# Selective scan on Trainium2: GpSimd's share of the products of B and du taken from transfers that spread du over the partitions, 5 of 16 in place of 1 of 3

## The reference, cut to what matters

```python
deltaA = exp(delta[..., None] * A)            # per direction, channel, state
deltaBx = (delta * u)[..., None] * B          # du times B
h = deltaA * h_before + deltaBx               # recurrence along L, 16 states
y = sum over states of h * C
```

## Time and profile before

| | us |
|---|---|
| median of 3 runs | 28245.57 (28242.69 to 28276.12) |
| the profiled execution, its own time | 28245.18 |
| its span, first to last instruction | 28243.4 |
| VectorE busy | 25430.9 (90%) |
| PE matmuls busy | 23025.3 (82%) |
| GpSimd busy | 22840.0 (81%) |
| ScalarE busy | 14594.0 (52%) |
| mean granted TensorE clock | 0.841 |

### The profile page before, as it was taken

How to read it: one execution, slowest core, us unless ns; L and a number is a source line. 1 busy time by engine, 2 the same in 40 slices (tenths; PEclk the granted TensorE clock), 3 DMA queues, 4 the chain that set the end, 5 groups by cost and what they waited for, 6 DMA issues and landing times. The chain is left out here.

```text
span 28243.4 us, 328050 instructions
## 1 busy us (share of the span) xinstructions
PE 23025.3 (82%) x97488; PEld 6748.7 (24%) x97488; DVE 25430.9 (90%) x16259; ACT 14594.0 (52%) x20088; POOL 22840.0 (81%) x10240
## 2 busy tenths in 40 slices
PE   8878888888766888888887888888885788888886
PEld 3322222222232222222233222222222322222222
DVE  2489999999779999999986999999997799999998
ACT  1265555555366555555514655555552655555553
POOL 0169999999147999999971799999990499999993
PEclk9978888888777888888868888888887788888888
DMA  2242221221454222222266422122216622222224
GB/s 87 93 140 49 49 49 40 49 49 42 161 201 155 46 43 49 49 46 43 49 226 220 124 49 49 40 49 49 49 44 223 212 49 49 45 44 49 49 45 150
DMA packets 1123929, 2332.74 MB, mean 83 GB/s; under 512 B 98486, under 2 KB 609426, under 8 KB 1113868
## 3 DMA queue, kind: packets, MB, share of 16 engines
q1 hardware_dynamic: 1120340, 2308.66, 30.0%
q10 hardware_dynamic: 1728, 1.70, 0.0%
HBM read 1329.40 MB, written 980.58 MB: 82 GB/s over the span
## 5 line engine op out<-in xcount | busy, mean ns | idle before, releaser
L1589 POOL TENSOR_TENSOR scan_hc<-scan_bc,scan_h 128x1024 f32<-128x1024 f32 x6912 | 16069.3, 2356 | 123.7 <-DVE scan_h L1766 122.5
L1766 DVE TENSOR_TENSOR_SCAN scan_h<-scan_da,scan_state,scan_dbu 128x1024 f32<-128x1024 f32 x6912 | 15981.4, 2336 | 155.5 <-ACT scan_da L1643 147.3
L1680 PE MATMUL scan_da<-scan_dd,scan_ssel 32*128 32x512 f32 x27648 | 9125.4, 746 | 2994.8 <-DVE scan_h L1766 2760.6
L1643 ACT ACTIVATE scan_da<-scan_da,scan_a_cur 128x1024 f32<-128x1024 f32 x6912 | 7516.3, 1087 | 7752.1 <-PE scan_da L1680 7747.5
L1680 PE MATMUL scan_p_du<-scan_dd,scan_ssel 32*128 32x512 f32 x27648 | 9216.0, 746 | 451.7 <-DVE scan_dbu L1753 168.3
L1753 DVE TENSOR_TENSOR scan_dbu<-scan_p_du,scan_bc 128x1024 f32<-128x1024 f32 x4608 | 5553.8, 1205 | 370.2 <-PE scan_p_du L1680 336.1
L1575 POOL TENSOR_TENSOR scan_dbu<-scan_bc,scan_dus 128x1024 f32<-128x1024 f32 x2304 | 5431.4, 2357 | 58.7 <-ACT scan_dus L1617 56.5
L1680 PEld LDWEIGHTS scan_da<-scan_dd,scan_ssel 32*128 32x128 f32 x27648 | 2459.0, 217 | 10302.3 <-DVE scan_h L1766 8710.9
L1697 PE MATMUL scan_p_y<-scan_hc,scan_rsel 128*32 128x512 f32 x27648 | 4789.5, 774 | 18.4 <-POOL scan_hc L1589 17.8
L1680 PEld LDWEIGHTS scan_p_du<-scan_dd,scan_ssel 32*128 32x128 f32 x27648 | 2418.2, 212 | 3521.2 <-DVE scan_dbu L1753 2934.2
L1622 ACT ACTIVATE scan_state<-scan_h,scan_a_cur 128x1 f32<-128x1 f32 x6912 | 2023.4, 293 | 1571.6 <-DVE scan_h L1766 1462.0
(11 more groups left out here) (220 smaller groups left out, 13404.0 us busy)
## 6 DMA issues: line engine op xcount, KB each, us to landing
scan_bc<-bc_d SPq DMA_DIRECT2D x576, 512.0 KB, 12.0
du_d<-prep_useq SPq DMA_DIRECT2D x384, 576.0 KB, 3.7
delta_d<-prep_delta SPq DMA_DIRECT2D x384, 576.0 KB, 4.5
y_d<-scan_y SPq DMA_DIRECT2D x576, 384.0 KB, 5.2
scan_dd<-delta_d SPq DMA_DIRECT2D x1136, 192.0 KB, 4.8
scan_dd<-du_d SPq DMA_DIRECT2D x1136, 192.0 KB, 6.5
fin_y<-y_d SPq DMA_DIRECT2D x288, 576.0 KB, 5.2
xs_d<-proj_xs_o SPq DMA_DIRECT2D x96, 588.0 KB, 3.3
```

The lines of the kernel that those rows point to most:

```text
L1589: nc.gpsimd.tensor_tensor(hc[:, u % HC_SLOTS, :], c, h[:, u % H_SLOTS, :], ALU.mult).then_inc(hc_ready, 1)
L1643: nc.scalar.activation(da[u % DELTA_BANKS][:], da[u % DELTA_BANKS][:], ACT.Exp, scale=a_cur[:, slot(u)[0], u % UNITS:u % UNITS + 1]).then_ ...
L1680: return nc.tensor.matmul(dst[:, half * H:(half + 1) * H], ssel[rows, i, :], dd[rows, s, m, j, :], start=True, stop=True)
L1766: nc.vector.tensor_tensor_scan(h[:, v % H_SLOTS, :], da[v % DELTA_BANKS][:], dbu[:, v % DBU_SLOTS, :], state[:, v % UNITS:v % UNITS + 1], ...
```

## The change

GpSimd's share becomes 5 units of every 16 (u % 16 in 2, 5, 8, 11, 14), 15 to a chunk in place of 16. VectorE makes the other 11 of 16, 33 to a chunk in place of 32. For a shared unit TensorE spreads nothing and ScalarE copies nothing: SyncE issues one DMA (`load_share`) that reads the unit's 8 rows of du, 1024 positions each, 16 times over and writes all 128 partitions of one of 5 slots of `dus` (512 KB). It is issued when the product that held the slot is done, 5 shares ahead. SyncE's list for a chunk is now a sequence of 15 such steps, each with its wait for a product of GpSimd. The store of the chunk before, and the loads of the chunk after, stand behind the step k = STORE_AT = 6. ScalarE's `keep`, exponential and `evacuate`, with its wait above, are as they were. Before the first chunk, 5 share loads stand between `load_first` and the other loads (`load_rest`).

```diff
-TRIO = 3
+TURN = 16
+SHARED = (2, 5, 8, 11, 14)
+ROUND_SHARES = ROUND // TURN * len(SHARED)
+ROUND_OWN = ROUND - ROUND_SHARES
+SHARE_AHEAD = 4
 DELTA_BANKS = 2
 DBU_SLOTS = 6
-DUS_SLOTS = 2
+DUS_SLOTS = 5
+CHUNK_SHARES = UNITS // TURN * len(SHARED)
+STORE_AT = 6
 H_SLOTS = 4
 HC_SLOTS = 8
 PAIR = 2
...
-    return u % TRIO == 2
+    return u % TURN in SHARED
+
+
+def shares(u):
+
+    return len(SHARED) * (u // TURN) + sum(s < u % TURN for s in SHARED)
+
+
+def share_unit(k):
+
+    return k // len(SHARED) * TURN + SHARED[k % len(SHARED)]
...
-        share_spread = ph.sem("share_spread")
-        share_copied = ph.sem("share_copied")
+        dus_loaded = [ph.sem(f"dus_loaded{b}") for b in range(DUS_SLOTS)]
+        freed = ph.sem("freed")
...
+                def load_rest():
...
                     sp.wait_ge(y_ready, c * EIGHTS + EIGHTS + ONE)
+                    sp.sem_inc(freed, 1)
                     for half in range(2):
                         for b in range(2):
                             sp.dma_start(y_d[b * 64:(b + 1) * 64, :, bass.ds(at + half * H, H)],
                                          y[half * 64:(half + 1) * 64, b::2, :]).then_inc(y_stored, 16)
+                def load_share(at, k):
+                    m, j, i = unit(share_unit(k % CHUNK_SHARES))
+                    first = j * QUAD + i * CPU
+                    sp.dma_start(dus[:, k % DUS_SLOTS, :],
+                                 du_d[first:first + CPU, m, bass.ds(at, T)].unsqueeze(0).broadcast_to([STATES, CPU, T])).then_inc(dus_loaded[k % DUS_SLOTS], 16)
+
+                def chunk(c, at, s, first, last):
+
+
+                    for k in range(CHUNK_SHARES):
+                        ahead = k + DUS_SLOTS
+                        if ahead < CHUNK_SHARES or not last:
+
+                            sp.wait_ge(share_ready, c * CHUNK_SHARES + (k + 1) + ONE)
+                            sp.sem_inc(freed, 1)
+                            load_share(at + ahead // CHUNK_SHARES * T, ahead)
+                        if k == STORE_AT and not first:
+                            store(c - 1, at - T)
+                            if not last:
+                                load(at + T, 1 - s)
...
                 load_first()
-                for s in range(1, CHUNK_SLOTS):
-                    load(s * T, s)
-                with sp.Fori(0, (ALL_CHUNKS - CHUNK_SLOTS) // CHUNK_SLOTS) as i:
+                for k in range(DUS_SLOTS):
+                    load_share(0, k)
+                load_rest()
+                load(T, 1)
+                chunk(0, 0, 0, True, False)
+                with sp.Fori(0, (ALL_CHUNKS - 2) // CHUNK_SLOTS) as i:
                     for s in range(CHUNK_SLOTS):
-
-                        store(i * CHUNK_SLOTS + s, i * (CHUNK_SLOTS * T) + s * T)
-                        load(i * (CHUNK_SLOTS * T) + (s + CHUNK_SLOTS) * T, s)
-                for s in range(CHUNK_SLOTS):
-                    store(ALL_CHUNKS - CHUNK_SLOTS + s, (ALL_CHUNKS - CHUNK_SLOTS + s) * T)
+                        chunk(i * CHUNK_SLOTS + (s + 1), i * (CHUNK_SLOTS * T) + (s + 1) * T, 1 - s, False, False)
+                chunk(ALL_CHUNKS - 1, (ALL_CHUNKS - 1) * T, 1, False, True)
+                store(ALL_CHUNKS - 1, (ALL_CHUNKS - 1) * T)
...
-                def share(r, u):
-                    g.wait_ge(share_copied, r * (ROUND // TRIO) + (u // TRIO + 1) + ONE)
+                def share(r, u, first=False):
+                    if first and u == SHARED[0]:
+                        g.wait_ge(first_loaded, FIRST_LOADS + ONE)
+                    elif u % UNITS == SHARED[0] or first and FIRST_UNITS <= u < FIRST_UNITS + SHARE_AHEAD:
+
+                        t, n = slot(u)
+                        g.wait_ge(loaded[t], r * (TURNS * LOADS) + n * LOADS + ONE)
+                    k = shares(u)
+                    g.wait_ge(dus_loaded[k % DUS_SLOTS], r * (ROUND_SHARES // DUS_SLOTS * 16) + (k // DUS_SLOTS + 1) * 16 + ONE)
                     g.wait_ge(scanned, nth(r * ROUND, u - DBU_SLOTS + 1) + ONE)
                     g.sem_inc(passed, 1)
                     s, _ = slot(u % ROUND)
                     nc.gpsimd.tensor_tensor(dbu[:, u % DBU_SLOTS, :], bc[:, s, image(u % UNITS), :],
-                                            dus[:, u // TRIO % DUS_SLOTS, :], ALU.mult).then_inc(share_ready, 1)
...
-                        ahead = u + TRIO + 1
+                        ahead = u + SHARE_AHEAD
                         if shared(ahead) and not (last and ahead >= ROUND):
-                            share(r, ahead)
+                            share(r, ahead, first)
...
-                for u in range(TRIO):
-                    if shared(u):
-                        share(0, u)
-                rounds(0, False)
+                share(0, SHARED[0], True)
+                rounds(0, True, False)
...
-                def copy_share(r, u):
-                    a.wait_ge(share_spread, r * (ROUND // TRIO) + (u // TRIO + 1) + ONE)
-
-                    a.wait_ge(share_ready, nth(r * (ROUND // TRIO), u // TRIO - DUS_SLOTS + 1) + ONE)
-                    nc.scalar.activation(dus[:, u // TRIO % DUS_SLOTS, :], p_du[:], ACT.Copy).then_inc(share_copied, 1)
...
-                        if shared(u) and not (last and u + TRIO >= ROUND):
-                            copy_share(r, u + TRIO)
...
-                def spread_share(r, u):
-                    spread(p_du, 1, u, 0)
-                    spread(p_du, 1, u, 1).then_inc(share_spread, 1)
...
-                        t.wait_ge(dbu_ready, r * (ROUND // TRIO * 2) + (u // TRIO * 2 + u % TRIO) + ONE)
                         if not shared(u):
-
-                            t.wait_ge(share_copied, r * (ROUND // TRIO) + (u // TRIO + 1) + ONE)
+                            t.wait_ge(dbu_ready, r * ROUND_OWN + (u - shares(u)) + ONE)
                             spread(p_du, 1, u, 0)
                             spread(p_du, 1, u, 1).then_inc(du_spread, 1)
-                        elif not (last and u + TRIO >= ROUND):
-                            spread_share(r, u + TRIO)
```

More of the change, by code:

```diff
@@ L1519, in _ @@
             def _(sp):
+                sources = [(n, src, half) for n, src in enumerate((delta_d, du_d)) for half in range(2)]
                 def load_first():
-                    sources = [(n, src, half) for n, src in enumerate((delta_d, du_d)) for half in range(2)]
                     for j in range(2):
@@ L1575, in share, with rounds @@
                     nc.gpsimd.tensor_tensor(dbu[:, u % DBU_SLOTS, :], bc[:, s, image(u % UNITS), :],
-                                            dus[:, u // TRIO % DUS_SLOTS, :], ALU.mult).then_inc(share_ready, 1)
-                def rounds(r, last):
+                                            dus[:, k % DUS_SLOTS, :], ALU.mult).then_inc(share_ready, 1)
+                def rounds(r, first, last):
                     q = r * ROUND
                     for u in range(ROUND):
-                        ahead = u + TRIO + 1
+                        ahead = u + SHARE_AHEAD
                         if shared(ahead) and not (last and ahead >= ROUND):
-                            share(r, ahead)
+                            share(r, ahead, first)
                         g.wait_ge(scanned, q + (u + 1) + ONE)
@@ L1662, in _ @@
                 a.wait_ge(zeroed, 1 + ONE)
-                for u in range(TRIO):
-                    if shared(u):
-                        copy_share(0, u)
                 rounds(0, True, False)
@@ L1730, in _ @@
                 t.wait_ge(first_loaded, FIRST_LOADS + ONE)
-                for u in range(TRIO):
-                    if shared(u):
-                        spread_share(0, u)
                 rounds(0, True, False)
@@ L1749, in times_b @@
                         d.wait_ge(loaded[s], r * (TURNS * LOADS) + n * LOADS + ONE)
-                    d.wait_ge(du_spread, r * (ROUND // TRIO * 2) + (u // TRIO * 2 + u % TRIO + 1) + ONE)
+                    d.wait_ge(du_spread, r * ROUND_OWN + (u - shares(u) + 1) + ONE)
                     d.wait_ge(scanned, nth(r * ROUND, u - DBU_SLOTS + 1) + ONE)
@@ L1759, in recur @@
                     if shared(u):
[L1760 removed]
+                        d.wait_ge(share_ready, r * ROUND_SHARES + (shares(u) + 1) + ONE)
                     else:
[L1762 removed]
+                        d.wait_ge(dbu_ready, r * ROUND_OWN + (u - shares(u) + 1) + ONE)
                     d.wait_ge(kept, nth(r * ROUND, u - H_SLOTS + 1) + ONE)
```

12 lines of the change are left out of this document (5 added, 7 removed).

## The result

The changed kernel takes **31,732 us** (median; 31,696 to 31,748) against 28,244: **1.1227** times as long, with a 95% interval of 1.1214 to 1.1241. The prediction was 30,630 with a range of 30,050 to 31,300: the sign is right, the size is short by 1102 us and lies outside the range. The profiled run's span is 31,732.2 us.

A forecast was written before the change was run, and what follows sets the result against it. GpSimd was taken to set the pace, VectorE right behind; a stopped chunk takes 145.0 + 17.8 + 2.5 = 165.3 us for 148.3. Over 140 chunks +2380, first chunks -7, starts +10: 30,630 us, range 30,050 to 31,300.

The forecast's parts named there:

- the stop: Before unit 17's recurrence, VectorE idles while ScalarE's copy at unit 16 waits for the late store: 17.8 us a chunk.
- The profile's signs: VectorE idle about 18 us 140 times, ScalarE's copy waiting on stores, stores after products, 2160 transfers, GpSimd 89% busy.
- The covers: Share 12's load has about 20 us to spare, the next chunk's loads arrive in time; layer starts lose 2.5 us each.
- After the stop: TensorE restarts at 1.2 GHz for some 12 units: 2 us a chunk, 2.5 with other waits, bounds 0.5 and 5.
- level with VectorE at the slow clock: TensorE at the slow clock, 10.75 matmul instructions a unit for 12, would need 3.04 us a unit, matching VectorE.
- waits that GpSimd's pace forces: In the kernel before, VectorE's 4.4 us a chunk beyond its 143.9 us of work, put down to GpSimd.
- VectorE's other waits: Waits of VectorE in a chunk apart from the stop and the slow clock following it: 0.5 us a chunk.
- cost it at nothing: ScalarE's 16 copies and TensorE's 16 of 96 spreads a chunk removed: both engines have room, so 0 us.
- The store was not in time: Rival, 6%: ScalarE's copy at unit 16 doesn't wait for unit 21's share; 146.5 us a chunk, 27,990 us.
- the stop was not short: Rival, 6%: stores land at the fast end and TensorE's slow clock costs nothing; 13.0 us more a chunk, 30,070 us.
- The du transfers come late: Rival, 4%: share 12 lands over 20 us later, so GpSimd also waits, 10 us a chunk; 32,070 us.

The follow-up runs named there:

- after: The changed kernel as described, its store behind the seventh share, against the kernel before: 31,732 us, 1.1227.
- store3: The changed kernel with the store and the next chunk's loads behind the fourth share instead of the seventh: 29,256 us, 1.0356.
- store3_spread: store3 with TensorE again spreading du of the shared units, with nobody to read it: 28,914 us, 1.0235.
- store3_copy: store3_spread plus ScalarE's copies of the shared units, made for nobody, and TensorE's wait for them: 28,696 us, 1.0150.
- copy5: The kernel before with five shares of 16, du still copied by ScalarE, no transfers, sums in their old place: 28,645 us.
- trio_dma: store3 with every third unit shared, as before the change, du still from transfers: 29,163 us.
- trio_dma_spread: trio_dma with TensorE's unread spreads of du for the shared units added: 28,968 us.
- trio_dma_copy: trio_dma_spread plus ScalarE's copies into a buffer nobody reads, with TensorE's wait for them: 28,356 us, 1.0037.
- trio_dma_act: trio_dma_spread plus ScalarE copies of the same width from a constant, with no wait of TensorE on them: 28,945 us.
- order: store3 with TensorE's sums behind delta's spread at units 1, 7 and 13 of 16: 28,516 us, 1.0094.
- before_order7: The kernel before with only TensorE's sums moved: behind delta's spread where a shared unit follows, 7 units behind for 9: 33,051 us, 1.1686.

## Why the prediction was short

The 3,488 us that the change costs come apart by these runs: the stop 2,476 (after less store3); TensorE's lighter list 342 (less store3_spread); ScalarE's copies gone and TensorE's wait with them 218 (less store3_copy); GpSimd's new source 51 (less copy5); the uneven row with 33 own products for 32, 401. The last two rest on one execution of copy5. The parts depend on the rest of the kernel: with every third unit shared, the lighter list costs 195 us (trio_dma less trio_dma_spread) and the copies with their waits 612.

**What held.** The stop, step by step: the seventh share behind the recurrence of 16, two products of GpSimd, 10.6 us from the share to the copy, ScalarE in front of the exponential; 17.16 us idle in the stop shown, 17.3 on average, 17.7 us a chunk by store3, for 17.8. Bytes at 222 GB/s with the start on top were a price that came out right. The sentence by the Trainium skill (DMA: Bandwidth & Descriptors, Anatomy of one DMA) gave 4.2 us less a stop, and this stretch doesn't bear it out: its DMA engines are 95% busy at 252 GB/s from 4080 to 4090. The skill fits that formula to single DMAs issued by GpSimd; these come in a row from SyncE. The profile's signs came: 140 waits of ScalarE's copy, stores behind a product, 2160 transfers. One didn't: GpSimd is busy 84% of a scan, not 89%, which was the sign of more waits than the stop. The covers held: GpSimd waits for its transfers 4 times, 51.0 us, at the starts of layers.

```profile
L1623 POOL TENSOR_TENSOR scan_dbu<-scan_bc,scan_dus 128x1024 f32<-128x1024 f32 x2160 | 5074.5, 2349 | 81.5 <-DMA scan_dus<-du_d 51.0 <-DMA scan_bc<-bc_d 30.5
```

**What failed is the term "After the stop"**, 2.5 us a chunk with bounds of 0.5 and 5. VectorE's two groups over the whole run (busy us, mean ns, then idle before them):

```profile
L1790 DVE TENSOR_TENSOR_SCAN scan_h<-scan_da,scan_state,scan_dbu 128x1024 f32<-128x1024 f32 x6912 | 16083.6, 2342 | 3441.7 <-ACT scan_da L1681 3421.9
L1777 DVE TENSOR_TENSOR scan_dbu<-scan_p_du,scan_bc 128x1024 f32<-128x1024 f32 x4752 | 5743.2, 1209 | 327.7 <-PE scan_p_du L1715 308.4
```

Of these 3769 us the 140 stops are 2424, and some 60 lie ahead of the first recurrences. The other 1285 us are **8.9** us a chunk, where 2.5 was forecast; store3 has 8.8 without any stop. That is some 930 of the 1102 us. Another 1.9 us a chunk, some 260 us, is VectorE's work, 146.9 for the 145.0 worked out from one calm stretch; the kernel before has 145.2 over its scans where the prediction made it 143.9. The stop took some 70 us less than forecast, and what lies outside the scans some 30 less.

Three steps led there. *The slow clock was put down to the stop and given 12 units after it.* After a stop it lasts some 10 us, in which VectorE hardly waits; the slow clock that costs stands all through the scan, and the lighter list is what took it from 0.83 to 0.72. *TensorE with a tenth less to do was called level with VectorE at the slow clock.* That took its work as a mean per unit. But VectorE waits for the exponential at single turns, those of units 1, 7 and 13, where du, sums and delta are 2.08 + 1.94 + 2.08 us one behind the other, and no removed spread stood in such a turn: in the kernel before they stand in the turns of the shared units. They also freed less than a mean says where they ran beside a spread of delta, for such a pair takes no longer than one spread alone: 2.09 us for both at the half clock, for 2.08. The timeline of the kernel before has both kinds:

```profile
4036.28 1.13 PE L1680 MATMUL scan_da<-scan_dd,scan_ssel 32*128 32x512 f32 x4 [1.13 <-DVE scan_h L1766]
4037.39 1.13 PE L1680 MATMUL scan_p_du<-scan_dd,scan_ssel 32*128 32x512 f32 x4
...
4040.00 1.22 PE L1680 MATMUL scan_da<-scan_dd,scan_ssel 32*128 32x512 f32 x2
4040.01 1.23 PE L1680 MATMUL scan_p_du<-scan_dd,scan_ssel 32*128 32x512 f32 x2
4041.01 1.06 PE L1680 MATMUL scan_da<-scan_dd,scan_ssel 32*128 32x512 f32 x2
4041.03 1.06 PE L1680 MATMUL scan_p_du<-scan_dd,scan_ssel 32*128 32x512 f32 x2
```

The two of a pair use different rows of the array (`rows` in `spread`). The Trainium skill (TensorE: Matmul & The Clock Gate, Part 3) says that matmuls on different row tiles run at the same time, and these lines agree. The pair is an own unit's du, unit 6 of its chunk; the line of 4037.39 is a shared unit's, and it ran alone. Most of the removed ones did: only 282 of 2300 ran beside delta's for over half of their time, for 2993 of the 4608 own ones. So the change took mostly lone spreads, from turns with room, and left the long turns as they were. *The other 4.4 us were called waits that GpSimd's pace forces.* Of VectorE's 93 idle us in the window of the kernel before (3.1 us a chunk over its four scans), 87 end with TensorE's spread of du or with the exponential behind delta's. GpSimd, busy 99% there, would bound the kernel near the same time without them. But these waits were there before any stop, and the term allowed 0.5 us for "VectorE's other waits". The earlier trace rows give busy time alone; what ends VectorE's idle time would have spoken against "cost it at nothing" for TensorE's lighter list.

**The rivals.** The store was not in time, the stop was not short. "The du transfers come late" gave 32,070, near the result, but by a mechanism that isn't there.

**Open** is why the copy and its waits lower VectorE's waits for TensorE. The runs show that they do, and that the clock rises with them. The traces show which spreads run beside delta's: with the waits (trio_dma_copy) 13% of the shared units' spreads overlap one by over a fifth of their time, without them 34% (trio_dma_spread) and 32% (trio_dma_act), while of the own ones 65% do with them, 61% without. That fits an unread spread which takes the place beside delta from one that VectorE needs, but no run tests it. Open too is by what rule a lighter list is granted a lower clock. Left over as well is the split of the uneven row's 401 us beyond the 170 of the product. No version run here beats the kernel before.

## What to carry over

A wait put into a queue in order is priced by walking the queue from what it waits for to what stands behind it; that gave the stop within 1 us. But work taken off an engine with room isn't free: ask in which of its turns the work stood, what the engine's slow level does to the longest row of its instructions between two handovers, and which waits go with the work. Compare the sums of a change against an ablation that puts the idle work back.

## What the runs showed that I had not expected

- Less work, lower clock, more time: 15 spreads of du a chunk fewer took the mean granted clock from 0.83 to 0.72 (store3_spread to store3) and cost 342 us. With half the sums' columns the clock was 0.53.
- A matmul list at 0.53 beat one at 0.72 by 264 us; its longest wait for the exponential was 0.8 us for 1.7.
- A clock brought back from 0.70 to 0.83 (trio_dma to trio_dma_spread) gave back only 195 of some 900 us.
- 16 copies a chunk that nobody reads, with the waits that tie them to TensorE, gained 612 us; copies of the same width without these waits 23.
- A DMA load of 104 GB/s beside the scan cost nothing: 28,247 for 28,268 us.
- The sums moved behind delta's spread gained 740 us in one kernel (order) and cost 4,800, together with a lag of 7 for 9, in another (before_order7).
